# Graph layer on one Trainium2 core: the preamble's block length, the order of its first loads, and the way of the degrees

## The reference

```python
edge_index = jnp.stack([src, dst])
h_self = x @ W_self.T + b_self
messages = x[src] @ W_neigh.T + b_neigh
h_neigh = jax.ops.segment_sum(messages, dst, num_segments=50000)
y = x + jax.nn.relu(h_self + h_neigh)
out = (y - mean(y)) / sqrt(var(y) + 1e-5)      # over the 128 features of a node
```

## Time and profile before

| | |
|---|---|
| Median of 3 runs | 678.21 us (675.71 to 680.98) |
| The profiled execution | 679.41 us |
| Its span in the profile | 677.6 us |
| Mean granted TensorE clock | 0.917 |
| Busy: PE, DVE, ACT, POOL | 76%, 62%, 52%, 60% |
| First matmul of trio 0's products | 59.54 us after the span's start |

### The profile page before, as it was taken

The page is one execution under the profiler, slowest core; times in us unless marked ns, Lnnn a source line. Parts: engine busy times, 40 slices in busy tenths (PEclk is TensorE's granted clock), DMA queues, the critical chain, the costliest instruction groups (busy, mean ns, idle before and its releaser), DMA issues.

```text
span 677.6 us, 12705 instructions
## 1 busy us (share of the span) xinstructions
PE 512.6 (76%) x3281; PEld 466.3 (69%) x3281; DVE 420.5 (62%) x1921; ACT 352.7 (52%) x1049; POOL 406.4 (60%) x424
## 2 busy tenths in 40 slices
PE   2045866887977978976977796978887878889883
PEld 0034756787867968866866696967776767778872
DVE  7884757587667677877557745445545543655554
ACT  1010354465655654654665655555655555656567
POOL 4776755666666665765666566566666666656610
PEclk9999897897997788999898988899999799889798
DMA  2522243354553563544544545444555454445433
GB/s 78 144 64 52 80 114 94 102 142 123 141 143 92 151 170 97 151 123 112 139 124 123 149 123 135 115 133 115 139 134 138 114 137 131 122 137 136 135 103 96
DMA packets 122942, 82.20 MB, mean 121 GB/s; under 512 B 15374, under 2 KB 115894, under 8 KB 122840
## 3 DMA queue, kind: packets, MB, share of 16 engines
q1 hardware_dynamic: 109208, 53.63, 28.4%
q0 software_dynamic: 13664, 27.77, 16.4%
HBM read 55.44 MB, written 26.71 MB: 121 GB/s over the span
## 4 chain that ended last, share of the span: by engine, by line
PE 50%; issue 20%; ACT 12%; another core or an unknown queue 6%; DVE 4%; DMA 3%; ACTq 2%; SPq 2%; POOL 1%; DVEq 0%
PE bank L890 17%; PE bank L913 11%; PE bank L914 9%; PE bank L878 6%; ACT result L1024 6%; PE bank L909 3%; ACT sums_t L997 3%; PE bank L895 3%; ACT x_t L1005 2%; DMA x_in<-in_x 2%; ACT std L1014 1%; ACTq L995 1%; DVE y L741 1%; DVE pick L731 1%
## 5 line engine op out<-in xcount | busy, mean ns | idle before, releaser
L483 POOL DMA_INDIRECT ring<-in_x,chunk_src x391 | 382.0, 977 | 229.9 <-issue 85.2
L741 DVE SCALAR_TENSOR_TENSOR y<-bank,x_in 128x384 f32<-128x384 f32 x131 | 72.5, 554 | 233.2 <-remote 114.5
L997 ACT COPY sums_t<-bank 128x192 f32 x391 | 125.2, 320 | 168.9 <-issue 45.0
L890 PE MATMUL bank<-pick,ring 128*128 128x193 f32 (+1 forms) x782 | 188.9, 370 | 10.6 <-DMA ring<-in_x,chunk_src 6.3
L913 PE MATMUL bank<-wsum_t,x_t 128*128 128x128 f32 (+1 forms) x782 | 175.7, 307 | 3.6 <-issue 3.6
L914 PE MATMUL bank<-wn_t,sums_t 128*128 128x128 f32 (+1 forms) x782 | 162.0, 290 | 7.1 <-issue 7.0
L1024 ACT ACTIVATE result<-y,minus_mean,rstd 128x128 f32<-128x128 f32 x391 | 162.9, 482 | 0.0
L890 PEld LDWEIGHTS bank<-pick,ring 128*128 128x128 f32 x782 | 142.2, 216 | 13.0 <-issue 12.7
L913 PEld LDWEIGHTS bank<-wsum_t,x_t 128*128 128x128 f32 (+1 forms) x782 | 126.8, 203 | 29.1 <-issue 29.0
L878 PE MATMUL bank<-identity,x_in 128*128 128x128 f32 x391 | 74.2, 304 | 92.5 <-issue 46.4
L914 PEld LDWEIGHTS bank<-wn_t,sums_t 128*128 128x128 f32 (+1 forms) x782 | 128.3, 206 | 8.5 <-issue 8.5
(11 more groups left out here) (118 smaller groups left out, 175.1 us busy)
## 6 DMA issues: line engine op xcount, KB each, us to landing
x_in<-in_x SPq DMA_DIRECT2D x130, 192.0 KB
out<-result SPq DMA_DIRECT2D x130, 192.0 KB
ring<-in_x,chunk_src POOLq DMA_INDIRECT x391
degrees_t<-degrees_dram SPq DMA_DIRECT2D x130, 2.2 KB
dst_padded<-in_dst SPq DMA_DIRECT2D x1, 390.6 KB
src_padded<-in_src SPq DMA_DIRECT2D x1, 390.6 KB
edge_src<-in_src SPq DMA_DIRECT2D x1, 390.6 KB
edge_dst<-in_dst SPq DMA_DIRECT2D x1, 390.6 KB
```

Source lines behind the costliest of these rows:

```text
L483: nc.gpsimd.indirect_dma_start(ring[:, c % RING, :], None, x, bass.IndirectOffsetOnAxis(ap=chunk_src[:, c:c + 1], axis=0)).then_inc(gather ...
L741: v.scalar_tensor_tensor(y[tau % DEEP][0:rows, 0:tiles, :], h_bank[b][0:rows, 0:tiles * DIM].rearrange("p (q d) -> p q d", q=tiles), 0.0, ...
L890: ins = mm(into[:, frame:frame + SPAN + carried], ring[:, c % RING, :], pick[tau % DEEP][:, c % TRIO, 0:SPAN + carried], start=(c == 0), s ...
L997: nc.scalar.copy(sums_t[:, bass.ds(at, SPAN)], sum_bank[c // PAIR % SUM_BANKS][:, frame:frame + SPAN]).then_inc(sums_placed, 1)
```

## The change

- `BLOCK` is 400 and `BLOCKS` 250: `end_dst`, `ends` and the comparisons of `find_blocks` have half as many elements, the fetched blocks and the comparisons in them twice as many.
- On GpSimd the block of a = 1 for column 0 is no longer fetched ahead of the windows of column 0; the four blocks of a = 1 come behind them, together.
- `window_landed` is split into `dst_landed` and `src_landed`, and `pack_start` into `pack_moves` (needs dst only) and `pack_words` (needs src). For column 0, `pack_moves` stands ahead of `find_rank_places(1, 4)` and `pack_words` behind it.
- `degrees_dram` and `store_degrees` are gone: `load_degrees` moves 3 partitions of `degrees`, each three times, from SBUF straight to the 9 rows of `degrees_t`. SyncE waits for `degrees_done` alone.
- SyncE's wait ahead of the bias transfers is for `src_landed[0]` alone.

```diff
-BLOCK = 200
+BLOCK = 400
...
-    below = [sb(f"below{j}", [SPREAD, BLOCKS]) for j in range(COLUMNS)]
+    below = [sb(f"below{j}", [SPREAD, max(BLOCK, BLOCKS)]) for j in range(COLUMNS)]
...
+                j, first = divmod(tau * TRIO, SPREAD)
                 sp.dma_start(degrees_t[tau % DEEP][0:tiles * PARTS, :],
-                             degrees_dram[tau * TRIO * PARTS:(tau * TRIO + tiles) * PARTS, :]).then_inc(degrees_landed[tau % DEEP], 16)
-
-            def store_degrees(part, j0, j1):
-
-                sp.wait_ge(degrees_done, part)
-                for j in range(j0, j1):
-                    sp.dma_start(degrees_dram[j * SPREAD * PARTS:(j + 1) * SPREAD * PARTS, :].rearrange("(p a) n -> p a n", a=PARTS),
-                                 degrees[:, j, :].unsqueeze(1).to_broadcast([SPREAD, PARTS, P])).then_inc(degrees_stored, 16)
-                sp.wait_ge(degrees_stored, 16 * j1)
+                             degrees[first:first + tiles, j, :].unsqueeze(1).to_broadcast([tiles, PARTS, P])).then_inc(degrees_landed[tau % DEEP], 16)
...
             sp.wait_ge(k.parts_made, 3)
-            sp.wait_ge(window_landed[0], 32)
+            sp.wait_ge(src_landed[0], 16)
...
-            store_degrees(1, 0, 1)
+            sp.wait_ge(degrees_done, 1)
...
                 if tau == FIRST_TRIOS:
-                    store_degrees(2, 1, 2)
+                    sp.wait_ge(degrees_done, 2)
...
                 if tau == 2 * FIRST_TRIOS:
-                    store_degrees(3, 2, COLUMNS)
+                    sp.wait_ge(degrees_done, 3)
...
             load_blocks(0, range(1, COLUMNS))
-            pool.wait_ge(blocks_found, 3)
-            load_blocks(1, [0])
             pool.wait_ge(padded_stored, 64)
             pool.wait_ge(places_found, 1)
             load_windows([0])
-            load_blocks(1, range(1, COLUMNS))
+            pool.wait_ge(blocks_found, 3)
+            load_blocks(1, range(COLUMNS))
...
-            def pack_start(j0, j1):
+            def pack_moves(j0, j1):
                 js, at = slice(j0, j1), slice(0, j1 - j0)
                 for j in range(j0, j1):
-                    dve.wait_ge(window_landed[j], 32)
+                    dve.wait_ge(dst_landed[j], 16)
...
                 link(ins)
+
+            def pack_words(j0, j1):
+                js, at = slice(j0, j1), slice(0, j1 - j0)
+                for j in range(j0, j1):
+                    dve.wait_ge(src_landed[j], 16)
                 link(v.scalar_tensor_tensor(words[1][:, at, :], src_window[:, js, :], 16, moves[:, at, :],
                                             ALU.logical_shift_left, ALU.bitwise_or))
...
+            pack_moves(0, 1)
             find_rank_places(1, COLUMNS)
-
-            pack_start(0, 1)
+            pack_words(0, 1)
             pack_bits(0, 1, range(0, 3))
```

More of the change, by code:

```diff
@@ L202, in build_common_case @@
     dst_padded = scratch("dst_padded", (EDGES + PAD, 1), INT32)
-    degrees_dram = scratch("degrees_dram", (ENTRIES * PARTS, P), BF16)
     edge_src = sb("edge_src", [EDGE_ROWS, EDGE_COLS], INT32)
@@ L246, in build_common_case @@
     offsets = sb("offsets", [1, ENTRIES + LOAD], INT32)
-    raw_at = sb("raw_at", [SPREAD, WINDOW])
+    raw_at = sb("raw_at", [SPREAD, BLOCK])
     kept_in_tile = sb("kept_in_tile", [SPREAD, COLUMNS])
@@ L290, in build_common_case @@
     places_found = sem("places_found")
-    window_landed = [sem(f"window_landed{i}") for i in range(COLUMNS)]
+    dst_landed = [sem(f"dst_landed{i}") for i in range(COLUMNS)]
+    src_landed = [sem(f"src_landed{i}") for i in range(COLUMNS)]
     tile_window_landed = [sem(f"tile_window_landed{i}") for i in range(COLUMNS)]
@@ L299, in build_common_case @@
     degrees_done = sem("degrees_done")
-    degrees_stored = sem("degrees_stored")
     dve_order = sem("dve_order")
@@ L433, in _ @@
             iota(k.partition[:], [[1, 1]], 1).then_inc(k.iotas, 1)
-            iota(raw_at[:], [[1, WINDOW]], 0).then_inc(k.iotas, 1)
+            iota(raw_at[:], [[1, BLOCK]], 0).then_inc(k.iotas, 1)
             iota(columns[:], [[1, SPAN + 2]], 0).then_inc(k.iotas, 1)
@@ L448, in load_windows @@
                 for j in js:
-                    for mine, padded in ((dst_window, dst_padded), (src_window, src_padded)):
+                    for mine, padded, landed in ((dst_window, dst_padded, dst_landed[j]), (src_window, src_padded, src_landed[j])):
                         nc.gpsimd.indirect_dma_start(mine[:, j, :], None, padded,
                                                      bass.IndirectOffsetOnAxis(ap=place_index[:, 0, j:j + 1], axis=0)
-                                                     ).then_inc(window_landed[j], 16)
+                                                     ).then_inc(landed, 16)
             def load_tile_windows(js):
@@ L530, in find_blocks @@
                 for j in range(j0, j1):
-                    ins = v.tensor_scalar(below[j][:], ends_bank[a][0:SPREAD, 0:BLOCKS],
+                    ins = v.tensor_scalar(below[j][:, 0:BLOCKS], ends_bank[a][0:SPREAD, 0:BLOCKS],
                                           limit[:, j:j + 1], 0.0, (ALU.is_le, ALU.is_lt)[a], ALU.add, accum_out=counts[:, a, j:j + 1])
@@ L541, in find_rank_places @@
                 v.tensor_tensor(dst_ahead[:, j0:j1, :], dst_block[:, 0, j0:j1, :],
-                                raw_at[:, 0:BLOCK].unsqueeze(1).to_broadcast([SPREAD, j1 - j0, BLOCK]), ALU.subtract)
+                                raw_at[:].unsqueeze(1).to_broadcast([SPREAD, j1 - j0, BLOCK]), ALU.subtract)
                 link(v.scalar_tensor_tensor(rank_bound[:, j0:j1], block[:, 0, j0:j1], float(BLOCK), limit[:, j0:j1], ALU.mult, ALU.subtract))
@@ L624, in degrees_start @@
                 for j in range(j0, j1):
-                    ins = v.scalar_tensor_tensor(moves[:, j - j0, :], tile_dst[:, j, 0:WINDOW], limit[:, j:j + 1], raw_at[:], ALU.subtract, ALU.subtract)
+                    ins = v.scalar_tensor_tensor(moves[:, j - j0, :], tile_dst[:, j, 0:WINDOW], limit[:, j:j + 1], raw_at[:, 0:WINDOW], ALU.subtract, ALU.subtract)
                 link(ins)
@@ L789, in later_lists @@
                 if t == 0:
-                    pack_start(1, 2)
+                    pack_moves(1, 2)
+                    pack_words(1, 2)
                 if 1 <= t < 9:
@@ L805, in later_lists @@
                 if t == 20:
-                    pack_start(2, COLUMNS)
+                    pack_moves(2, COLUMNS)
+                    pack_words(2, COLUMNS)
                 if 21 <= t < 37 and t % 2:
```

## The result

| | before | changed |
|---|---|---|
| Median | 678.89 us (4 runs, 675.71 to 680.98) | 688.46 us (4 runs, 682.82 to 693.01) |
| Ratio, 95% interval | | 1.0115 (1.0072 to 1.0157) |
| The profiled execution, its span | 679.41, 677.6 us | 687.08, 685.3 us |
| First products on PE | 59.54 us | 55.96 us |

The kernel became slower by 1.15%, where 0.6% faster was forecast. The start gained about what was forecast, and the main loop lost three times as much.

What follows compares the result with a forecast made beforehand. No engine fills the span; the degrees alone set the main loop's start. Saving 1.45 us upstream plus 2.5 on the degrees transfer, say 3.9, gives 674.3 us from the 678.21 median (675.5 profiled); range 668.5 to 679.5.

Steps and rivals of the forecast that it cites:

- The start: Preamble up to first products: 1.45 us gained until degrees are done, 2.5 on their transfer; first products near 55.6.
- The loop keeps a head start: Main loop: its start is set by the degrees alone, so each us earlier moves the whole loop.
- the rival in which the head start is used up: Main loop gives the 3.9 us back, waiting for POOL or the edges' load: 678.2, no change; chance 0.17.
- the ring: POOL's gathers before the main loop: read as having gone as far ahead as allowed, then idle 2.84 us.
- The rest: Remaining terms: two later stores' removal costed at nothing; 0.27 us longer issue for 131 degrees transfers stays on SyncE.
- The sum: Whole kernel: 1.45 us upstream plus 2.5 on the degrees transfer, 3.95, say 3.9 us saved.
- The slower rival: New transfer clogs SyncE's queue behind the edges: 5.1 us later there, total 679.4, up to 688; chance 0.08.
- PE's record: First products end near 62.9, y starts at 66.96; the sum stands if that 4 us gap moves with the start.
- The dearer stops: Rival: without SyncE's stops, x_in and degrees_t come earlier at 207 to 248 us; 9.5 saved, 668.7; chance 0.15.
- the two stops: SyncE standing 2.8 us at each of two later degrees stores, at 207.20 and ahead of trio 66.

Runs made afterwards that it cites:

- preamble half: Changed kernel with degrees again stored to DRAM and loaded from there, against the kernel before: 669.83 against 672.60 us, ratio 0.9972.
- degrees half: Kernel before with only the degrees moved within SBUF: 680.02 against 672.60 us, ratio 1.0110; repeated on another chip, 685.80 against 673.07, ratio 1.0176.
- e3_spare_dram_two: Kernel before plus two unread spare transfers per trio of the old form (9 rows, one piece in DRAM): 683.83 us, ratio 1.0017.
- e3_degrees_first: Kernel before with degrees moved within SBUF, from trio 6 on issued ahead of the trio's x load: 692.97 us, ratio 1.0176.
- e3_spare_sbuf: Kernel before plus one unread spare SBUF transfer per trio (3 rows, each three times): 698.47 against 681.73 us, ratio 1.0209.
- e1_first_six: Changed kernel with only the first six degrees transfers within SBUF, later ones through DRAM, against the kernel before: 669.48 against 672.60 us, ratio 0.9945.

## Why the prediction was wrong

**The start: right.** The forecast put the first products near 55.6; they came at 55.96. `end_dst` saved 1.26 us (0.7 taken, 0 to 1.4 allowed). `dst_window` was issued at 12.53 (12.7). The word began at 20.30 (20.5), DVE waited 1.47 ahead of `flag` (1.2), `degrees` was done 1.95 earlier (1.45), and the transfer within SBUF took 2.48 us from issue to matmul where I took 1.6, near the upper end of its bounds; it saved 1.6, not 2.5. That the start came within 0.4 us is in part luck: 0.5 us more was gained ahead of `degrees`, 0.9 less behind it. Block loads landed 3.3 us after their issue against 2.8, covered as forecast.

**The loop keeps a head start: right.** The preamble half gains 1.75 us at the first products and 0.28% (1.9 us) at the end; with six transfers in SBUF it gains 3.4 us and 0.55% (3.7 us). The intervals are wide beside this (no change to 0.6% for the one, 0.2% to 0.9% for the other), but the second excludes the rival in which the head start is used up. One reading behind that rival was wrong: at 59.54 POOL had not yet filled the ring. In the trace of the kernel before it gathers without a pause until 65.08, and only then stands still, for the 2.84 us.

**The step that failed:** under "The rest", the sentence that a longer issue of 0.27 us for 131 transfers stays on SyncE, beside its waits. It does stay on SyncE, and yet each such transfer costs the loop 0.07 to 0.1 us (1.10% and 1.76% measured for the degrees half, that is 7.5 and 12 us, with a head start of 1.7 us inside). The sum put this term at nothing because nobody waits for SyncE, and no more was asked. The changed kernel's total follows from the halves: 0.9972 times 1.0110 to 1.0176 is 1.008 to 1.015, against 1.0115.

**The slower rival: right in what it blamed, wrong in the rest.** It named the new transfer's form. But it put the cost at one place, behind the edges, where the lead changed by only 0.4 us net (trios 30 to 40, against 5.4 between trios 80 and 90), and through SyncE's time, against which e3_spare_dram_two speaks: two issues more per trio cost nothing that can be told from 0. Its price of 1.2 us net and a chance of 0.08 came from that. Its upper end of 688 is near the measured 688.46, but by luck, since it stands on the same mechanism. The rule of "DMA: Bandwidth & Descriptors" of the Trainium skill, section "Rules for kernel authors", on few leading rows does not settle it. Three rows of 256 bytes cost 2.38% and sixteen, which would spread over all engines, 0.82%; that is its direction. But sixteen still cost, nine rows from SBUF cost like three (1.77% and 1.1% to 1.76%), and nobody waits for the landing that it would delay.

**PE's record.** The prediction set aside a gap of 4 us between the end of the first products' records and their `y`, and assumed that it would move along with the start. It did not. It was 4.1 us before and is 0.6 us in the changed kernel (58.68 and 0.63 against 59.87), so the first `y` came 7.1 us earlier and not 3.9; by trio 5 only 2.2 us of this were left. In the other traces of the slower chips the stretch from the first products to the first `y` is anywhere from 3.5 to 10.1 us, and in all four of the faster chip 3.5. So on the slower chips the end of PE's record is no sure sign of when `y` can start. That this is what bounds the loop there is argued, not shown.

**The dearer stops.** No run takes the two stops away alone. In the changed kernel they are gone, and its chain still holds 10.00 us of an `x_in` load at 238.53, where it was 11.60 before. e3_degrees_first, without the stops, and e3_spare_sbuf, with them, have one transfer of the new form per trio on the same chip. They differ by 0.33%, 2.2 us, of which the earlier start explains 1.7. So nothing like 5.6 us is seen, but intervals of 0.6% and more leave room for a part of it.

The best version measured is e1_first_six: new blocks and order, six transfers within SBUF, the rest through DRAM, 0.55% faster than the kernel before (0.2% to 0.9%).

## What to carry to other kernels

Time the halves of a change apart: a small gain at the start and a small loss per turn of a loop look like one number. In this kernel the form to keep for the transfer that is repeated in the loop was the one with the short issue (one piece in DRAM, 0.45 us or less), and the direct way within SBUF was worth having only where somebody waits for it. When many waits end in signals that no record explains, the profile does not show the whole bound, and a term that seems to touch nobody should be measured, not costed at nothing.

## What the runs showed of the hardware

- The same program takes 566 us on one chip and 672 to 682 us on four others; one with a spare transfer took 567.9 and 688.7. A difference of 1% can be read only between runs on one chip.
- A transfer of 2.2 KB per trio that nobody waits for cost 2.1% of the kernel in one form, and two of another form together cost 0.17% (-0.2% to 0.5%), on a chip of the slower kind. 0.8 KB in three pieces cost 2.4% on another of that kind and 0.3% on the faster chip.
- A DMA issue of 0.8 to 2.2 KB within SBUF takes longer on SyncE (0.69 to 0.75 us) than the issue of a 192 KB load (0.48 us).
